# New order of the jobs between the second MLP and the last attention, and the low parts of q and k on GpSimd

## The chip, the cores and the metric

One NeuronCore of a Trainium2 chip runs the whole program. The time is the device time of one execution in microseconds (us); of several executions the median counts. TensorE (PE), VectorE (DVE), ScalarE (ACT), GpSimd (POOL) and SyncE (SP) each work through their own instruction list in order and wait for one another by semaphores. SP only issues DMAs here, and POOL issues some as well.

## The reference, cut to what matters

Four conditional layers on x of 2 batches x 1024 tokens x 256 features, float32. The change lies between the MLP of the second layer and the attention of the fourth:

```python
# end of layer 1: MLP
h = gelu(h @ mlp_w1 + mlp_b1) @ mlp_w2 + mlp_b2 ; x = x_in + h
# layer 2: adapters of rank 8 (a1, bb1, a2, bb2 from the condition)
y = einsum('btd,bdr->btr', x, a1); y = einsum('btr,bdr->btd', y, bb1)
y = gelu(y)
y = einsum('btd,bdr->btr', y, a2); y = einsum('btr,bdr->btd', y, bb2)
x = y + x
# layer 3: norm, 16 heads of 16 features
h = gamma * layernorm(x) + beta
q, k, v = h @ Wqkv.T + bqkv
att = softmax(q @ k.T) / 16 ; out = (att @ v) @ Wp.T + bp ; ...
```

## The kernel before

The order of all work is one list, `SCHED` (lines 86 to 161), of pairs (stage, number). Every engine has a function for the stages in which it takes part, and `run` calls them in the order of the list, so an engine's instruction list is the list of stages cut to its own part. The order on each engine is thus fixed, and a wait holds up all that stands behind it on that engine.

The stages around the change, all of them once for batch 0 and once for batch 1:

- `u1`, `d1`: up and down matmuls of the MLP (L1352, L1374). Batch 1's `d1` parts 24 to 31 are the last. `d1` on POOL adds a bias to X (L800), on DVE adds the result (L2012).
- `x2`: X turned by 16 transposes (L1293), copied by ACT (L1083). `a1`, `g`, `a2`, `f2`: the adapter chain (L1486, L1504, L1486, L1515). ACT copies `a1` and `a2` (L1128) and takes the gelu of `g` (L1133). For `f2` DVE adds four banks to X (L2113) and takes statistics (L1774, L1777), POOL makes the reciprocal deviations (L794, L795), and `fn` normalises on DVE (L1785).
- `n3`: XN turned (L1293). ACT writes each of four tiles twice (L1068), once rounded to float32r as the high part and once whole, and DVE subtracts for the low part (L2134).
- `qk3` j: one tile (128 features x 512 tokens) of q or k, six matmuls (L1529) of three products of high and low parts. Eight jobs for batch 0 (0 to 7), eight for batch 1 (8 to 15). ACT writes the high part (L1123), DVE the low part from the same PSUM bank (L2122) into `PARTS`, which holds four jobs, and two DMAs (L579, L580) store 512 and 256 KB in DRAM: from SP for jobs 0 to 7, from POOL for 8 to 15.
- `v3` j: 12 matmuls (L1540), copied by ACT into `VP` (L1076). Four jobs for each batch.
- `mx` n: two matmuls (L1578) of the pass that finds the row maxima of the scores, reduced by one DVE instruction (L2157). The two pairs of banks in PD alternate, so `mx` n waits until n-2 is reduced. The first 26 (`LEAD`) are done before the first `step`, the other 230 in the steps. `tm` turns a unit's maxima, and SP spreads them (L731).
- `bt`, `bm`: a bias row through the projection. POOL pads `VP` with memsets (L885, L888) in `x2` of batch 1.
- `step` n, 128 of them: energies (L1607), exponentials on ACT (L1154), the sum with the values (L1618), and two `mx`.

Jobs that go through the four banks of PA, all but `mx`, `tm` and the down matmuls, take them in turn: each waits until the job four before it in the list has been evacuated. `g` and `f2` ask for all their four banks before their first matmul.

SP's list has its own order: store jobs 0 to 3; stack 0 (`stack(1)`, four DMAs from DRAM into `STKR`, L700, which wait until jobs 0 to 3 are stored); rows of ones (L708); wait for the MLP's end; stack 1; store jobs 4 to 7; ones; stack 2 (waits until jobs 4 to 7 are stored); ones; then the maxima for the steps. `mx` 0 waits for stack 0. ACT waits before `qk3` j (j of 4 and more) until job j-4 is stored.

## Time and profile before

| what | value |
| --- | --- |
| median of 3 runs | 880.11 us (878.17 to 881.54) |
| the profiled execution | 879.38 us, span 877.5 us |
| mean granted clock of TensorE | 0.977 |
| PE busy | 828.5 us, 94% of the span |
| DVE busy | 682.6 us, 78% |
| ACT busy | 471.6 us, 54% |
| POOL busy | 227.9 us, 26% |
| last down matmul of the second MLP to first energy of the steps | 439.8 to 506.1 us |

How to read it: busy time is summed over an engine's instructions. PE's matmuls are pipelined, so that a record is longer than the distance to the next one. The distance between starts is what a matmul costs. The granted clock is a share of full speed (2.4 GHz at 1.0, 1.2 GHz at 0.5). All positions in time are us from the start of the span.

### The profile page before, as it was taken

The numbers are of one execution on the slowest core, as the hardware profiler recorded it, in microseconds if no ns is written. First come the engines' busy times: TensorE is split into PE (matmuls) and PEld (weight loads), VectorE is DVE, ScalarE is ACT, GpSimd is POOL, SyncE is SP. The second block draws the span as 40 slices with busy tenths as digits, with TensorE's granted clock in tenths as the row PEclk, the third lists the DMA queues.
The fourth block names the chain that finished last, engine by engine and source line by source line (L and its number), as shares of the span: only waits on it lengthen the run. The fifth ranks groups of instructions, "written<-read, shape, count | busy, mean of one in ns | idle before, by whom it ended". The sixth has DMA issues, their size and how long they took to land.

```text
span 877.5 us, 13593 instructions
## 1 busy us (share of the span) xinstructions
PE 828.5 (94%) x5112; PEld 537.5 (61%) x5112; DVE 682.6 (78%) x1155; ACT 471.6 (54%) x857; POOL 227.9 (26%) x377
## 2 busy tenths in 40 slices
PE   5999999999999999997988989999999999999994
PEld 3668888988987998886856633333333433333342
DVE  7998657779558568648358869999999999999377
ACT  4746232243342452343234257888888788888760
POOL 4443412203003003112012620333333333333411
PEclk9999999999999999999989969999999999999996
DMA  8613122110000000000596700505050405010002
GB/s 314 252 49 97 51 96 99 49 53 1 1 1 1 1 1 1 1 1 1 174 201 158 264 1 3 92 21 92 21 93 21 92 21 98 23 25 21 27 25 73
DMA packets 29381, 57.42 MB, mean 65 GB/s; under 512 B 7228, under 2 KB 15152, under 8 KB 29314
## 3 DMA queue, kind: packets, MB, share of 16 engines
q1 hardware_dynamic: 22596, 44.40, 19.4%
q0 software_dynamic: 6720, 12.15, 4.7%
q8 instruction: 41, 0.67, 0.3%
q14 instruction: 24, 0.20, 0.1%
HBM read 39.26 MB, written 14.91 MB: 62 GB/s over the span
## 4 chain that ended last, share of the span: by engine, by line
PE 80%; DVE 11%; ACT 5%; issue 2%; DMA 1%; POOL 1%; SPq 0%; DVEq 0%; ACTq 0%
PE PA L1607 15%; PE PA L1618 15%; PE PD L1374 10%; PE PA L1352 8%; PE PD L1578 7%; PE PA L1463 5%; PE PD L1432 4%; PE PA L1419 3%; PE PA L1529 2%; PE PD L1676 2%; PE PA L1540 2%; PE PA L1293 1%; DVE NMX L2157 1%; PE PA L1453 1%; DVE ST L1774 1%
## 5 line engine op out<-in xcount | busy, mean ns | idle before, releaser
L2157 DVE TENSOR_REDUCE NMX<-PD 128x2 f32<-128x1024 f32 x256 | 302.1, 1222 | 29.2 <-PE PD L1578 24.7
L1154 ACT ACTIVATE R<-PA 128x512 f32<-128x512 f32 x512 | 267.4, 604 | 72.8 <-PE PA L1607 71.2
L1607 PE MATMUL PA<-STKR 50*128 50x512 f32 x512 | 186.1, 455 | 3.8 <-ACT R L1154 2.7
L1607 PEld LDWEIGHTS PA<-STKR 50*128 50x128 f32 x512 | 83.1, 188 | 153.1 <-ACT R L1154 138.8
L1578 PE MATMUL PD<-STKR 48*128 48x512 f32 x512 | 150.2, 456 | 3.3 <-DVE NMX L2157 3.3
L1090 ACT ACTIVATE R<-PA,VEC 128x512 f32<-128x512 f32 x64 | 43.9, 689 | 102.9 <-PE PA L1352 90.4
L1374 PE MATMUL PD<-WHR,HSR 128*128 128x256 f32 x512 | 95.0, 285 | 0.5 <-DVE HSR L1994 0.5
L1374 PEld LDWEIGHTS PD<-WHR,HSR 128*128 128x128 f32 x512 | 82.1, 191 | 5.8 <-issue 1.6
L1352 PE MATMUL PA<-XSR,WHR 128*128 128x512 f32 x256 | 81.1, 398 | 3.9 <-issue 2.0
L1578 PEld LDWEIGHTS PD<-STKR 48*128 48x128 f32 x512 | 62.4, 188 | 21.9 <-DVE NMX L2157 10.9
L1374 PE MATMUL PD<-WLR,HSR 128*128 128x256 f32 x256 | 72.4, 283 | 0.0
L1993 DVE CAST HSR<-R 128x512 fp32r<-128x512 f32 x64 | 28.4, 444 | 56.2 <-ACT R L1090 56.2
L1618 PE MATMUL PA<-R 128*32 128x512 f32 x512 | 70.8, 626 | 0.0
L1618 PE MATMUL PA<-R,W 128*32 128x512 f32 x512 | 68.2, 605 | 0.0
L1352 PEld LDWEIGHTS PA<-XSR,WHR 128*128 128x128 f32 x256 | 45.5, 190 | 14.4 <-issue 7.0
L1994 DVE TENSOR_TENSOR HSR<-R,HSR 128x512 fp32r<-128x512 f32 x64 | 51.8, 810 | 2.2
L800 POOL TENSOR_TENSOR X<-X,BC 128x256 f32<-128x256 f32 x48 | 35.3, 756 | 65.0 <-DVE HSR L1994 53.3
L1352 PE MATMUL PA<-XSR,WLR 128*128 128x512 f32 x128 | 49.9, 390 | 0.0
L1374 PEld LDWEIGHTS PD<-WLR,HSR 128*128 128x128 f32 x256 | 48.9, 191 | 0.0
L1463 PE MATMUL PA<-VR,PTR 128*128 128x256 f32 x384 | 48.3, 284 | 0.0
L1463 PEld LDWEIGHTS PA<-VR,PTR 128*128 128x128 f32 x384 | 47.3, 191 | 0.6
L1102 ACT ACTIVATE R<-PD,NMS 128x1024 f32<-128x1024 f32 x16 | 17.9, 1117 | 54.2 <-DVE NMS L2066 54.1
(326 smaller groups left out, 1268.3 us busy)
## 6 DMA issues: line engine op xcount, KB each, us to landing
STKR<-qk_terms SPq DMA_DIRECT2D x32, 384.0 KB, 8.7
R<-in_l_w SPq DMA_DIRECT2D x8, 1024.0 KB, 5.1
W<-in_w SPq DMA_DIRECT2D x4, 1024.0 KB, 10.2
qk_terms<-PARTS SPq DMA_DIRECT2D x8, 512.0 KB, 3.4
qk_terms<-PARTS POOLq DMA_DIRECT2D x8, 512.0 KB, 3.4
S<-row_reciprocals POOLq DMA_DIRECT2D x56, 64.0 KB, 2.1
X<-in_x SPq DMA_DIRECT2D x4, 512.0 KB, 8.9
qk_terms<-PARTS SPq DMA_DIRECT2D x8, 256.0 KB, 4.5
```

What stands on the lines that cost most here:

```text
L800: i = po.tensor_tensor(x, x, row, ALU.add)
L1090: act.activation(dst, bank(b, tag, c, f_), func, bias=vec(bias, f_)).then_inc(s_aev, 1)
L1154: act.activation(PB[:, n % 2, j, :], PA[:, e % NEB, :], ACT.Exp).then_inc(s_exp3, 1)
L1352: m = pe.matmul(o, parts[w][:, k, f_ * P:(f_ + 1) * P], XS[:, c, x, k, :], start=(n == 0), stop=(n == len(terms) - 1))
L1374: m = pe.matmul(PD[:, (n + t) % 4, 0:D], HS[:, x, f_, t * P:(t + 1) * P], parts[w][:, f_, :], start=(f_ == 0 and (w, x) == TERMS[0]), stop ...
L1432: m = pe.matmul(PDF[:, t % 2, c * HALF:(c + 1) * HALF], QT[q][:, k, t * P:(t + 1) * P], KT[x][:, k, c * HALF:(c + 1) * HALF], start=(n == ...
L1463: m = pe.matmul(o[:, 0:D], PTR[:, x, t % NTURN, kt * P:(kt + 1) * P], V[v][:, kt, :], start=(n == 0), stop=(n == len(terms) - 1))
L1578: i = pe.matmul(PD[:, o + h, :], QS[rows, slot(gg), jj, q0:q0 + P], KS[rows, slot(gg), jj, kc * HALF:(kc + 1) * HALF], start=True, stop=True)
L1607: pe.matmul(PA[:, e % NEB, :], KS[rows, slot(gg), jj, kt * P:(kt + 1) * P], QS[rows, slot(gg), jj, c * HALF:(c + 1) * HALF], start=True, s ...
L1618: i = pe.matmul(PA[32 * j:32 * j + 32, 3, :], VP[b][:, kt, g_ * GH + j, :], PB[:, step % 2, j, :], start=(kt == 0), stop=(kt == NT - 1))
L1994: ve.tensor_tensor(lo, src, hi, ALU.subtract).then_inc(s_split, 1)
L2157: ve.tensor_reduce(out, PD[:, o:o + NROW, :], axis=AX_X, op=ALU.max, negate=True).then_inc(s_mred, 1)
```

## The change

Six edits:

1. Batch 0's `qk3` 0 and 1 come after `d1` 25 and `qk3` 2 and 3 after `d1` 26; before they came after `d1` 23 and 24. `n3` of batch 0 stays behind `d1` 23.
2. Between the MLP and batch 1's `n3` the list has a new order. `v3` 0 stands ahead of `g`, `v3` 1 and 2 ahead of `n3`, `v3` 3 after it; 5 `mx` instead of 9 stand ahead of `n3`.
3. Among `qk3` 8 to 15 there are two `mx` behind each job (before, one or two), and no `mx` is left behind the last `v3` pair.
4. ACT writes each job's q or k twice, the high part and the whole value; POOL subtracts the high part from the whole one in place. DVE has no part in `qk3`.
5. SP stores all 16 jobs. Jobs 8 to 13 stand behind stack 2 and its ones, jobs 14 and 15 behind the first spread of the maxima.
6. The high part of batch 1's `n3` has a buffer of its own (`XH1`); the padding of `VP` is a stage of its own (`vp`) behind `qk3` 7.

```diff
-               NTILE + 5: [("fn", 0)], NTILE + 7: [("n3", 0), ("qk3", 0), ("qk3", 1)],
-               NTILE + 8: [("qk3", 2), ("qk3", 3)]})
+               NTILE + 5: [("fn", 0)], NTILE + 7: [("n3", 0)], NTILE + 9: [("qk3", 0), ("qk3", 1)],
+               NTILE + 10: [("qk3", 2), ("qk3", 3)]})
...
-SCHED += [("x2", 1), ("qk3", 4), ("a1", 1), ("bt", 0), ("g", 1), ("qk3", 5), ("mx", 0), ("bm", 0), ("qk3", 6), ("mx", 1), ("a2", 1), ("mx", 2), ("mx", 3),
-          ("f2", 1), ("qk3", 7), ("mx", 4), ("v3", 0), ("mx", 5), ("v3", 1), ("fn", 1), ("mx", 6), ("v3", 2), ("mx", 7), ("v3", 3),
-          ("mx", 8), ("n3", 1)]
-EARLY = 9
+SCHED += [("x2", 1), ("qk3", 4), ("a1", 1), ("bt", 0), ("v3", 0), ("g", 1), ("mx", 0), ("mx", 1), ("qk3", 5), ("bm", 0), ("a2", 1),
+          ("qk3", 6), ("f2", 1), ("mx", 2), ("fn", 1), ("mx", 3), ("qk3", 7), ("vp", 0), ("v3", 1), ("v3", 2), ("mx", 4), ("n3", 1),
+          ("v3", 3), ("mx", 5)]
+EARLY = 6
...
-    SCHED += [("qk3", QJOBS + j), ("mx", EARLY)]
-    EARLY += 1
-    if EARLY >= UNIT + 2 and ("tm", 0) not in SCHED:
-        SCHED.append(("tm", 0))
-    elif j % 2 and j < QJOBS - 1:
+    SCHED.append(("qk3", QJOBS + j))
+    for i in range(2):
+        if EARLY >= UNIT + 2 and ("tm", 0) not in SCHED:
+            SCHED.append(("tm", 0))
         SCHED.append(("mx", EARLY))
         EARLY += 1
...
+            XH1 = at("XH1", R0 + 12288, [P, KB, T])
...
-        X3 = [[XH0[:, :, :], XTR[:, 0]], [XTR[:, 0], XTR[:, 1]]]
+        X3 = [[XH0[:, :, :], XTR[:, 0]], [XH1[:, :, :], XTR[:, 1]]]
...
                 for j in jobs:
-                    evacuated(sp, *qk3_job(j))
+                    sp.wait_ge(s_low3, j + 1)
                     store_parts(sp, j)
...
             ones_rows(2)
+            store(range(QJOBS, 2 * QJOBS - 2))
             for m in range(NUNIT):
...
+                if m == 0:
+                    store(range(2 * QJOBS - 2, 2 * QJOBS))
...
             def qk3(j):
-                if j >= QJOBS:
-                    evacuated(po, *qk3_job(j))
-                    store_parts(po, j)
+                high, low = parts(j)[:, 0], parts(j)[:, 1]
+                evacuated(po, *qk3_job(j))
+                po.tensor_tensor(low, low.bitcast(F32), high.bitcast(F32), ALU.subtract).then_inc(s_low3, 1)
...
-                act.activation(parts(j)[:, 0], full_bank(b, tag, side, c, k), ACT.Identity,
-                               bias=vec(("q3_b", "k3_b")[side], k)).then_inc(s_hi, 1)
+                o = bank(b, tag, side, c, k)
+                for dst in (parts(j)[:, 0], parts(j)[:, 1].bitcast(F32)):
+                    i = act.activation(dst, o, ACT.Identity, bias=vec(("q3_b", "k3_b")[side], k))
+                i.then_inc(s_aev, 1)
```

## Rows read from the trace of the kernel before

**Rows 1.** Stretches of 4 us: busy per engine, granted clock, DMA share, GB/s

```profile
416.00:420.00 4.00, 4.00 (x13) 3.14 (x12) 1.36 (x3) 0.69 (x2) 0.00 (x0) 0.63 0.06 17
...
440.00:444.00 4.00, 4.00 (x39) 2.87 (x36) 0.57 (x3) 2.76 (x5) 3.85 (x3) 1.00 1.04 160
...
456.00:460.00 4.00, 2.62 (x21) 1.80 (x22) 4.00 (x6) 0.00 (x0) 0.00 (x0) 0.75 1.04 386
...
512.00:516.00 4.00, 4.00 (x20) 1.64 (x16) 2.15 (x3) 2.10 (x4) 0.00 (x0) 0.50 0.02 6
...
528.00:532.00 4.00, 4.00 (x27) 1.33 (x27) 3.75 (x4) 3.41 (x7) 0.00 (x0) 1.00 0.00 0
```

**Rows 2.** PE in order of time, MLP's end: start, length, line, [idle before, releaser]

```profile
415.66 0.47 PE L1529 MATMUL PA<-XH,WQH 128*128 128x512 f32 x1 [4.03 <-DVE XSR L2134]
...
439.84 1.91 PE L1293 MATMUL PA<-ident,X 128*128 128x128 f32 x16
```

**Rows 3.** The chain that ended last, `qk3` 0 to 3: start, us, what

```profile
415.66 4.29 PE PA L1529 x12
...
425.80 2.75 PE PA L1529 x12
```

**Rows 4.** ACT in order of time: last evacuation of batch 0's `n3`

```profile
415.02 0.81 ACT L1068 ACTIVATE XT<-PA,PAR 128x512 f32<-128x512 f32 x1
```

**Rows 5.** PE in order of time, 445 to 506 us

```profile
445.19 1.15 PE L1504 MATMUL PA<-R,LB 8*128 8x256 f32 x16 [0.70 <-DVE DG L2137]
...
456.26 1.15 PE L1515 MATMUL PA<-LB,R 8*128 8x256 f32 x16
...
475.89 0.74 PE L1529 MATMUL PA<-XSR,WQH 128*128 128x512 f32 x2 [2.29 <-DVE XSR L2134]
...
487.94 0.50 PE L1578 MATMUL PD<-STKR 48*128 48x512 f32 x2
488.37 0.72 PE L1529 MATMUL PA<-XSR,WQH 128*128 128x512 f32 x2
...
489.92 0.50 PE L1578 MATMUL PD<-STKR 48*128 48x512 f32 x2
...
501.87 0.49 PE L1578 MATMUL PD<-STKR 48*128 48x512 f32 x2
...
503.92 0.73 PE L1578 MATMUL PD<-STKR 48*128 48x512 f32 x4
...
506.07 0.69 PE L1607 MATMUL PA<-STKR 50*128 50x512 f32 x3
```

**Rows 6.** DVE in order of time: adds of `f2`, and `fn`

```profile
457.96 2.48 DVE L2113 TENSOR_TENSOR X<-PA,X 128x512 f32<-128x512 f32 x4
...
466.73 2.67 DVE L1785 TENSOR_SCALAR XN<-X,MV,RST 128x256 f32<-128x256 f32 x8
```

**Rows 7.** The reductions of all `mx`, from the page: busy, mean ns

```profile
L2157 DVE TENSOR_REDUCE NMX<-PD 128x2 f32<-128x1024 f32 x256 | 302.1, 1222 | 29.2 <-PE PD L1578 24.7
```

**Rows 8.** POOL by line and shape: its two operations on 128 x 512

```profile
L911 POOL TENSOR_TENSOR S<-UO,S 128x512 f32<-128x512 f32 x7 | 8.9, 1276 | 12.5 <-DMA S<-row_reciprocals 12.5
...
L876 POOL TENSOR_TENSOR R<-R,S 128x512 f32<-128x512 f32 x4 | 7.1, 1776 | 12.8 <-DVE R L1956 12.8
```

**Rows 9.** DVE's subtraction L1994 in 404 to 430 us: ns min/median/max

```profile
L1994 DVE TENSOR_TENSOR HSR<-R,HSR x6: 693/693/1107, 406.6 to 425.8; 128x512 fp32r<-128x512 f32 x6
```

**Rows 10.** POOL beside the longest of these, in order of time

```profile
425.50 0.85 POOL L800 TENSOR_TENSOR X<-X,BC 128x256 f32<-128x256 f32 x1 [1.09 <-DVE HSR L1994]
```

**Rows 11.** SP's DMA issues of stacks 0 and 1, in order of time

```profile
434.29 1.76 SPq L700 DMA_DIRECT2D STKR<-qk_terms  x4
...
440.03 6.81 SPq L700 DMA_DIRECT2D STKR<-qk_terms  x4
```

**Rows 12.** DMA issues from the page (KB each, us to landing)

```profile
STKR<-qk_terms SPq DMA_DIRECT2D x32, 384.0 KB, 8.7
```

**Rows 13.** Landing times of all stores of L579

```profile
DMA to landing us min/median/max: 2.8/3.4/11.2
```

More of the change, by code:

```diff
@@ L265, in evacuations @@
     for _, tag, *_ in jobs:
-        by_dve = int(tag in ("ad", "gc", "wt", "wv", "q", "k", "v1", "p", "o", "qk3", "f2", "bt", "bm"))
+        by_dve = int(tag in ("ad", "gc", "wt", "wv", "q", "k", "v1", "p", "o", "f2", "bt", "bm"))
         seen[by_dve] += 1
@@ L528, in build @@
         s_exp1 = sem("probs1_ready")
-        s_hi = sem("qk_high_ready")
+        s_low3 = sem("qk_low_ready")
         s_w3high = sem("last_attention_weights_high_ready")
@@ L881, in x2, with v_padding @@
                     po.memset(ONES[:, :].bitcast(F32), 1.0).then_inc(s_ones, 1)
-                    return
+            def v_padding(_):
                 po.wait_ge(s_dfull, DJ[(1, "w21", NT - 1)] + 1)
@@ L930, in _ @@
                  "d0": prebias_in_mlp(0, lambda b: BG[:, b, :]), "h0": normed("h0", 1e-6, rms=True), "att": att,
-                 "pr": normed("pr", 1e-6, rms=True), "d1": prebias_in_mlp(1, lambda b: BC[:, MB2, :]), "x2": x2,
+                 "pr": normed("pr", 1e-6, rms=True), "d1": prebias_in_mlp(1, lambda b: BC[:, MB2, :]), "x2": x2, "vp": v_padding,
                  "f2": normed("f2", 1e-5), "qk3": qk3, "step": step, "end": normed("end", 1e-5)})
@@ L2114, in f2 @@
                 stats(b, lambda h: evacuated(ve, b, "f2", 2 * h + 1))
-            def qk3(j):
-                b, tag, side, c, k = qk3_job(j)
-                n = AJ[(b, tag, side, c, k)]
-                high, low = parts(j)[:, 0], parts(j)[:, 1]
-                bias = VC[("q3_b", "k3_b")[side]] + k
-                ve.wait_ge(s_hi, j + 1)
-                ve.scalar_tensor_tensor(low, PA[:, n % 4, :], VEC[:, bias:bias + 1], high.bitcast(F32), ALU.add,
-                                        ALU.subtract).then_inc(s_aevd, 1)
             def last_weights(_):
@@ L2236, in _ @@
                  "ao": att("ao"), "pr": pr, "d1": d1,
-                 "f2": f2, "fn": lambda b: normalise("f2", b, True), "qk3": qk3, "n3": last_halves, "w3": last_weights, "bt": bias_turned, "bm": bias_projected, "mx": reduce_max,
+                 "f2": f2, "fn": lambda b: normalise("f2", b, True), "n3": last_halves, "w3": last_weights, "bt": bias_turned, "bm": bias_projected, "mx": reduce_max,
                  "tm": turned_max, "step": step, "hd": heads_turned, "hx": heads_back, "p3": p3, "st": last_stats, "ea": end_scaled, "eb": end_sum})
```

## The prediction

> **What bounds the kernel now.** I read the stretches of 4 us first. TensorE is busy nearly everywhere except in one transition, from the end of the second MLP to the first energy, and in one hole ahead of it. From 416 to 420 it works at a mean clock of 0.63, and a later stretch holds only 2.62 us of work in 4 [rows 1]; there are several such. Next, PE in order of time: batch 0's n3 has ended at 411.6, and the next matmul starts at 415.66, after 4.03 us of idle, because qk3 0 needs the halves that ACT and DVE make from n3. The MLP ends and x2 starts at 439.84; the first energy is at 506.07 [rows 2, 5]. So the transition takes 66.2 us. From 506 on, the program is a fixed chain of 128 steps that the change leaves alone, so an earlier first energy is worth its full amount at the end, unless the clock there differs.
>
> **Term A: qk3 0 to 3 behind d25 and d26.** Three up jobs and two down parts now follow n3. The two spots of qk3 show the price of the clock: 12 matmuls took 4.29 us after the hole and 2.75 us without one [rows 3], so the hole costs 4.03 + 1.5 us. The cover is not perfect: u28 needs the bank of n3's first tile. ACT's n3 work of eight passes ends at 415.83 at 0.66 us a pass [rows 4], so the first two passes are done at 411.8, when PE has left the transposes; some 0.3 us stay. The up jobs of 1.38 us (six matmuls at 0.229) then just meet the other banks. Gain about 5.4 (4.5 to 5.8): x2 at 434.4.
>
> **Term B: x2 to f2.** Before, f2 started 16.4 us after x2 (439.84 to 456.26) [rows 2, 5]. Now x2 (1.66), qk3 4 (1.37), a1 (1.0), bt and v3 0 follow until 440.6. g asks for four banks and the last is v3 0's, so it starts when ACT has copied v3 0, 441.5, 0.9 idle, where before it started 5.35 after x2 [rows 5], which would be 439.8 now. Then mx 0 needs stack 0. Stores 2 and 3 follow ACT's two passes and POOL's subtraction and are ready at 427.5 and 428.9; with 768 KB each at 386 GB/s, 2.0 us [rows 1], stack 0 is issued near 433.0, against 434.29 [rows 11]. A stack is 4 x 384 KB [rows 12], at 160 GB/s [rows 1] 9.8 us, and it lands near 444.5. PE reaches mx 0 at 442.6: 1.9 idle, a wait that did not exist, and all of PE's list is behind it. Then mx 0, mx 1, qk3 5, bm, a2, qk3 6, some of it at half clock after these gaps: a2 near 450, qk3 6 ends at 451.6. f2's last bank is qk3 6's, which ACT frees after two passes (0.7 + 0.66), so f2 starts at 453.4 (452.6 to 455). That is 19 us after x2: this part loses 2.6. The gain so far is 2.9.
>
> **Term C: f2 to fn's end.** Before: 456.26 to 469.40, 13.1 us [rows 5, 6]. Adds and statistics take 7.0 us after f2's start (DVE then turned to the low part of qk3 7 at 463.8, which was 7.5 after f2; without a pause between add and add 7.0); then stood that low part (0.7) and two reductions, now one. With one reduction of 1.2 [rows 7] and fn's 2.7 [rows 6] the new time is 10.9. POOL has room: its rstd works sit ahead of qk3 7's low part. Gain 2.2; fn ends at 464.3.
>
> **Term D: fn's end to qk3 8.** Before 6.5 us (to 475.89, of them 2.29 idle) [rows 5, 6], while ACT and DVE turned n3 into halves. Now v3 3 and mx 5 stand in that wait. PE: last half of n3 0.8, v3 3 1.6, mx 5 0.4, and up to 1.5 for half clock (the hole of 4.03 cost that much [rows 3]; PE is idle near 460 to 461 and 462 to 464 waiting for mx 2's reduction and fn). The halves needed by qk3 8 are ready at 467.8. So qk3 8 starts at 468.6, 4.3 after fn: gain 2.2 (1.5 to 3).
>
> **Term E: qk3 8 to the first energy.** Before 30.2 us (475.89 to 506.07). A job takes 1.55 on PE and an mx 0.43 (487.94, 488.37, 489.92 [rows 5]). Two reductions on DVE take 2.44 at 1.222 each, a little less back to back [rows 7]. PE needs 1.55 + 0.43 + 0.43 = 2.41, with the second mx waiting until the reduction of the pair before has ended. The two chains are about equal, and I take 2.43 us a job. 8 x 2.43 = 19.4, tm 0.3, then four v3 and mx at 2.05 (501.87 to 503.92 [rows 5]) 8.2, and 0.3 for the last evacuation: 28.2. The mx pairs that stood behind v3 7, from 503.92 to the first energy at 506.07, are gone; but three mx and one v3 more follow n3 than before. Gain 2.0 (0 to 3).
>
> Sum: 5.4 - 2.6 + 2.2 + 2.2 + 2.0 = 9.2, so the first energy at 496.8. In the profiled execution 879.38 - 9.2 = 870.2; the median stood 0.73 above the profiled one, so 870.9.
>
> **What is costed at nothing.** *POOL's low part.* No row shows this operation on 128 x 512. The nearest, a product on 128 x 512, takes 1.28 us beside DVE's reductions and 1.78 in another place [rows 8]. Against a period of 2.43 both fit. I take 1.35; a faster one gains nothing, for nobody on PE waits for it. It would have to exceed 2.4 to set the pace. *ACT's second pass* (0.66) has room in 2.43, and its cost at f2 is in term B. *DVE* loses 16 low parts of 0.75, which is what makes room for two reductions. *SP.* Store 7 is ready at 463, lands at 466, stack 2 is issued then and lands at 477; stores 8 to 11 follow in the same queue at 2.0 each (479.5, 481.6, 483.6, 485.7). ACT wants job 8 stored at 479.7 for qk3 12, and job 11 at 487 for qk3 15, so waits are 0.6 at most and PE has four banks of room. The spread of the maxima lands near 490, needed at 496.8. *vp* (4.4 us on POOL at 463 to 467) is ahead of low part 8, needed at 471.5.
>
> GpSimd beside DVE: DVE's subtraction of 0.693 took 1.107 beside an add on POOL at its longest [rows 9, 10]. The Trainium skill, "GPSIMD Engine Reference", section 8 "Key points", says that the two share SBUF interfaces and collide for DVE instructions in a two-port mode or with two SBUF inputs. By that rule fn's and n3's operations beside low 7 and vp would be stretched by up to 0.4 each for the overlapped two or three, the trace agrees, and the sum would be 0.5 to 1 smaller: 871.6. The reductions read PSUM and keep 1.22, so I leave it in the range.
>
> **Rivals.**
>
> *Clock at the steps.* In the first steps, as at 512 to 516, PE works at clock 0.50 though it is busy throughout: 20 matmuls in 4 us, where 528 to 532 has 27 [rows 1]. That lasts to about 522, some 12 us that give a quarter less, and PE's waits for the first exponentials stand ahead of it. Estimate from these counts: 3 to 4.5 us lost. The new end of the transition has less idle; if the clock stays, 866.4. Against: the waits for the first exponentials stay. Chance 0.15.
>
> *A smaller gain: the queue.* Stores 4 to 7 are behind stack 1, 8 to 13 behind stack 2, all in SP's queue. A stack issue was held 6.81 us [rows 11], and stores behind one landed after 11.2 instead of 3.4 [rows 13]. If store 7 is late by 4 us (chain or POOL's list), stack 2 lands at 481, job 11 at 490, qk3 15 is evacuated at 491.5 and the end moves by 3 to 4 us: 874.5. The same size comes from a clock at half through most of 445 to 470. Chance 0.23. The Trainium skill, "DMA: Bandwidth & Descriptors", section "Issuing engines are not separate DMA queues", says that DMAs of all issuers run on the same 16 engines and interleave, so that a second issuer saves only issue time. By it moving the stores costs nothing but POOL's 1.3 us; in the trace a store behind a stack in one queue waits it out, and no row shows one from POOL beside a stack.
>
> *No change.* Only the MLP hole is won and the waits at mx 0, g, f2 and fn eat it: 876 to 884. Chance 0.08.
>
> *Slower.* More and longer gaps (1.9 at mx 0, 1.5 at f2, 1.6 and 1 at mx 4 and n3) leave the clock at half when the dense part starts, and it stays there as in 510 to 522. PE's 2.41 a job nearly doubles, 4.2 (1.8 more), and v3 with its mx goes from 2.05 to 3.4 (1.4 more). Over the whole stage 14.4 + 5.6 = 20, so 890.9. It decides from seven to eight jobs on: 9.2 + 4.4 = 13.6, over 1.8. Against: the fall behind the hole of 4.03 was over by 420, for the 12 matmuls at 425.80 ran at full price [rows 3]. Chance 0.05.
>
> **How the numbers follow.** The forecast holds 0.49, 868 to 873.5 around 870.9. A measurement can tell 0.5% here (4.4 us), so faster is below 875.7. With the clock case 0.15 and most of the queue case, faster 0.83; same 0.11; slower 0.06. The range leaves out the last two cases: 865.5 to 876.
>
> **What would show it.** No idle over 1 us on PE behind n3 of batch 0 and x2 at 434 to 435 (A). PE idle ahead of mx 0 with a DMA as releaser, and f2 at 452.6 to 455 (B). fn's end 11 us after f2 (C). Less than 0.5 idle ahead of qk3 8 (D). Jobs 8 to 15 at 2.4 us, POOL's L-line at 1.3 to 1.8 us (E). First energy at 495 to 499. The prediction falls if PE waits inside jobs 8 to 15 for ACT or a store, if POOL's subtraction takes over 2.4 us, or if the steps are slower than 2.5 us after the start.

## The result and the profile after

The changed kernel takes 873.53 us (median of 20 runs, 872.63 to 877.29), the kernel before 877.90 us in the 20 runs beside it (874.47 to 881.54). The ratio is 0.9957, 95% interval 0.9942 to 0.9971: faster by 0.43%, less than half of the 1.0% that was forecast (870.9), inside the range, and by its ratio just on the "no change" side of the 0.5% bound, which had a chance of 0.11. In two of the kernels below, e7 and e10, one disturbed run is in the count and the median, and not in the ratio. The profiled execution has a span of 871.3 us at a mean clock of 0.984, where the one of before had 877.5 at 0.977.

The page of the changed kernel, with its busy times:

```profile
span 871.3 us, 13609 instructions
PE 824.4 (95%) x5112; PEld 536.8 (62%) x5112; DVE 675.7 (78%) x1139; ACT 479.6 (55%) x873; POOL 237.9 (27%) x377
```

DVE has lost 7 us, ACT and POOL have gained 8 and 10, as the change says. PE has lost 4, though it does the same matmuls; the mean clock is higher (0.984 against 0.977). Now the transition, PE in order of time, the rows that answer to [rows 2, 5] (start, length, [idle before it, releaser]):

```profile
411.81 0.70 PE L1358 MATMUL PA<-XSR,WHR 128*128 128x512 f32 x2 [0.32 <-ACT XT L1072]
...
434.37 1.91 PE L1299 MATMUL PA<-ident,X 128*128 128x128 f32 x16
441.29 1.15 PE L1510 MATMUL PA<-R,LB 8*128 8x256 f32 x16 [0.84 <-ACT R L1080]
444.98 1.22 PE L1584 MATMUL PD<-STKR 48*128 48x512 f32 x4 [2.54 <-DMA STKR<-qk_terms]
454.98 1.15 PE L1521 MATMUL PA<-LB,R 8*128 8x256 f32 x16 [1.51 <-ACT PARTS L1129]
...
469.14 3.67 PE L1299 MATMUL PA<-ident,XN 128*128 128x128 f32 x16 [5.45 <-DVE XN L1791]
...
475.60 0.50 PE L1535 MATMUL PA<-XH,WQH 128*128 128x512 f32 x1
...
504.71 0.70 PE L1613 MATMUL PA<-STKR 50*128 50x512 f32 x3 [0.46 <-ACT W L1080]
```

Read against the forecast's five terms (L1584 is `mx`, L1521 `f2`, L1299 `x2` and `n3`, L1535 `qk3`, L1613 the energy):

| stretch | before | forecast | after | gain forecast | gain measured |
| --- | --- | --- | --- | --- | --- |
| A: start to `x2` | 439.84 | 434.4 | 434.37 | 5.4 | 5.5 |
| B: `x2` to `f2` | 16.4 | 19.0 | 20.6 | -2.6 | -4.2 |
| C: `f2` to the end of `fn` | 13.1 | 10.9 | 15.4 | 2.2 | -2.3 |
| D: end of `fn` to `qk3` 8 | 6.5 | 4.3 | 5.2 | 2.2 | 1.3 |
| E: `qk3` 8 to the first energy | 30.2 | 28.2 | 29.1 | 2.0 | 1.1 |
| first energy at | 506.07 | 496.8 | 504.71 | 9.2 | 1.4 |

The transition gave 1.4 us instead of 9.2; the span is shorter by 6.2. The other 4.8 lie behind the first energy, in steps that the change leaves alone. So there are two questions: where the transition's 7.8 us went, and where the steps' 4.8 came from.

DVE at `fn` in the changed kernel, the rows that answer to [rows 6], and POOL beside it:

```profile
461.95 1.19 DVE L2154 TENSOR_REDUCE NMX<-PD 128x2 f32<-128x1024 f32 x1
463.06 7.32 DVE L1791 TENSOR_SCALAR XN<-X,MV,RST 128x256 f32<-128x256 f32 x8
470.30 2.35 DVE L2154 TENSOR_REDUCE NMX<-PD 128x2 f32<-128x1024 f32 x2
```

```profile
463.44 1.25 POOL L897 TENSOR_TENSOR PARTS<-PARTS 128x512 fp32r<-128x512 f32 x1
464.64 1.79 POOL L889 MEMSET R<- 128x2048 f32 x1
466.49 0.34 POOL L892 MEMSET R<- 128x128 f32 x1
466.69 1.85 POOL L889 MEMSET W<- 128x2048 f32 x1
468.60 0.34 POOL L892 MEMSET W<- 128x128 f32 x1
```

The eight instructions of `fn` took 2.67 us before [rows 6] and take 7.32 now. They have the same operands, and DVE waits for nobody: its records are long. The times of a single one, of the changed kernel by line in 455 to 475 us (ns min/median/max):

```profile
L1791 DVE TENSOR_SCALAR XN<-X,MV,RST x8: 395/402/3205, 463.1 to 470.0; 128x256 f32<-128x256 f32 x8
```

and the two long ones, in order of time:

```profile
463.38 3.21 DVE L1791 TENSOR_SCALAR XN<-X,MV,RST 128x256 f32<-128x256 f32 x1
466.51 2.18 DVE L1791 TENSOR_SCALAR XN<-X,MV,RST 128x256 f32<-128x256 f32 x1
```

Five take 0.4 us, one 0.48, one 2.18 and one 3.21. The long ones end at 466.59 and 468.69, each 0.15 us after the end of a large memset (466.44 and 468.54), and the one of 0.48 ends 0.15 after the last small memset. From 463.44 to 468.94 POOL works almost without a break, 5.5 us, and `fn` grew by 4.65. PE stands for 5.45 us ahead of `n3`, and then works at half clock. The stretches of the changed kernel, columns as in [rows 1]:

```profile
444.00:448.00 4.00, 3.02 (x9) 2.02 (x9) 2.19 (x2) 0.48 (x1) 0.00 (x0) 0.53 0.88 151
448.00:452.00 4.00, 4.00 (x24) 2.18 (x23) 0.59 (x2) 1.31 (x3) 1.27 (x1) 0.62 1.05 167
...
464.00:468.00 4.00, 0.00 (x0) 0.00 (x0) 4.00 (x2) 0.00 (x0) 3.94 (x4) 1.00 0.53 197
468.00:472.00 4.00, 2.85 (x14) 2.86 (x15) 4.00 (x8) 1.70 (x3) 0.88 (x2) 0.51 0.78 138
472.00:476.00 4.00, 4.00 (x20) 3.57 (x19) 2.74 (x5) 4.00 (x7) 0.00 (x0) 0.63 1.01 154
...
508.00:512.00 4.00, 4.00 (x19) 1.52 (x19) 2.33 (x2) 2.29 (x6) 0.91 (x2) 0.63 0.00 0
512.00:516.00 4.00, 4.00 (x30) 1.67 (x26) 3.72 (x4) 3.49 (x8) 0.00 (x0) 0.94 0.01 4
```

From 464 to 468 DVE is busy for 4.00 us with two instructions. Twice a wait of PE is followed by 1.2 GHz (0.53 and 0.51). The last two lines are the steps: PE is close to full clock from 512 on (0.94), where before showed 0.50 at 512 [rows 1] and still

```profile
516.00:520.00 4.00, 4.00 (x20) 1.64 (x16) 2.29 (x3) 2.10 (x4) 0.00 (x0) 0.50 0.00 0
520.00:524.00 4.00, 4.00 (x21) 1.68 (x17) 2.47 (x4) 2.10 (x4) 0.00 (x0) 0.64 0.00 0
```

(the kernel before, same columns). In 4 us PE started 20 matmuls there, and 30 in the changed kernel.

### The profile page after: what moved, and what is told of

Its sections match the earlier page's. It is cut to its first block, busy times and chain, and to the rows that moved or that the text cites. A ratio compares the mean times of both kernels' runs of the same rounds, so it can differ in the third digit from the quotient of the medians.

```text
span 871.3 us, 13609 instructions
## 1 busy us (share of the span) xinstructions
PE 824.4 (95%) x5112; PEld 536.8 (62%) x5112; DVE 675.7 (78%) x1139; ACT 479.6 (55%) x873; POOL 237.9 (27%) x377
## 4 chain that ended last, share of the span: by engine, by line
PE 79%; DVE 10%; ACT 4%; DMA 2%; issue 2%; POOL 1%; SPq 1%; DVEq 0%; ACTq 0%
PE PA L1613 15%; PE PA L1624 15%; PE PD L1380 9%; PE PA L1358 8%; PE PD L1584 7%; PE PA L1469 5%; PE PD L1438 4%; PE PA L1425 3%; PE PA L1535 2%; PE PA L1299 2%; PE PD L1682 1%; PE PA L1459 1%; DVE ST L1780 1%; DMA STKR<-qk_terms 1%; PE PA L1546 1%
## 5 line engine op out<-in xcount | busy, mean ns | idle before, releaser
L1613 PE MATMUL PA<-STKR 50*128 50x512 f32 x512 | 183.8, 449 | 4.2 <-ACT R L1160 2.7
L1613 PEld LDWEIGHTS PA<-STKR 50*128 50x128 f32 x512 | 81.9, 185 | 151.3 <-ACT R L1160 141.8
L1584 PE MATMUL PD<-STKR 48*128 48x512 f32 x512 | 148.1, 452 | 3.0 <-DMA STKR<-qk_terms 2.5
L1584 PEld LDWEIGHTS PD<-STKR 48*128 48x128 f32 x512 | 60.7, 186 | 22.2 <-DVE NMX L2154 9.0
```

What stands on the lines that cost most here:

```text
L1584: i = pe.matmul(PD[:, o + h, :], QS[rows, slot(gg), jj, q0:q0 + P], KS[rows, slot(gg), jj, kc * HALF:(kc + 1) * HALF], start=True, stop=True)
L1613: pe.matmul(PA[:, e % NEB, :], KS[rows, slot(gg), jj, kt * P:(kt + 1) * P], QS[rows, slot(gg), jj, c * HALF:(c + 1) * HALF], start=True, s ...
```

## The experiments

Theory 1: what is missing from the transition is DVE's `fn` beside GpSimd's work (C), and `mx` 0, which waits for its stack (B). Theory 2: the order is at its limit, and something else becomes late where one of these is mended. For the steps: their length follows the clock in their first 24 us, which only e7's edit aims at.

| kernel | median (runs) | ratio to before, 95% | first energy | span behind it | clock, first 12 us and next 12 |
| --- | --- | --- | --- | --- | --- |
| before | 877.90 (20) | | 506.07 | 371.4 | 0.63, 0.80 |
| after | 873.53 (20) | 0.9957 (0.9942 to 0.9971) | 504.71 | 366.6 | 0.86, 1.00 |
| e1 | 870.27 (7) | 0.9928 (0.9901 to 0.9954) | 499.90 | 368.6 | 0.72, 1.00 |
| e2 | 872.99 (8) | 0.9942 (0.9920 to 0.9963) | 499.67 | 371.4 | 0.62, 0.81 |
| e3 | 878.17 (12) | 1.0007 (0.9987 to 1.0028) | 508.68 | 367.3 | 0.72, 1.00 |
| e4 | 871.52 (11) | 0.9942 (0.9918 to 0.9966) | 500.47 | 367.0 | 0.86, 1.00 |
| e5 | 867.29 (6) | 0.9893 (0.9862 to 0.9924) | 496.75 | 370.1 | 0.72, 1.00 |
| e6 | 876.68 (12) | 0.9991 (0.9968 to 1.0015) | 504.98 | 369.4 | 0.67, 0.90 |
| e7 | 877.38 (12) | 1.0004 (0.9973 to 1.0035) | 507.32 | 365.7 | 1.00, 1.00 |
| e8 | 876.83 (12) | 0.9990 (0.9973 to 1.0007) | 507.90 | 369.8 | 0.67, 0.91 |
| e10 | 866.28 (6) | 0.9880 (0.9848 to 0.9913) | 497.00 | 368.5 | 0.58, 0.99 |
| e11 | 862.88 (5) | 0.9838 (0.9813 to 0.9863) | 493.80 | 367.2 | 0.86, 1.00 |
| e12 | 874.81 (12) | 0.9967 (0.9947 to 0.9987) | 504.93 | 366.9 | 0.86, 1.00 |

The last three columns are of the one profiled execution; "first energy" is the start of the first matmul of the steps, the clock that of two stretches of 12 us from there. The intervals of neighbouring kernels often overlap (after, e1, e2, e4 and e12 do), so what one edit is worth is read from the first energy, and the total only supports it. The first energy has its own scatter: in the six kernels whose lists are alike up to `x2` (after, e1, e4, e5, e10, e11) it starts between 433.74 and 434.89, so a difference below about 1 us says nothing.

**e1, the changed kernel with the padding written early**, while DVE and GpSimd are both free:

```diff
-SCHED += [("x2", 1), ("qk3", 4), ("a1", 1), ...
-          ("qk3", 6), ("f2", 1), ("mx", 2), ("fn", 1), ("mx", 3), ("qk3", 7), ("vp", 0), ("v3", 1), ...
+SCHED += [("x2", 1), ("vp", 0), ("qk3", 4), ("a1", 1), ...
+          ("qk3", 6), ("f2", 1), ("mx", 2), ("fn", 1), ("mx", 3), ("qk3", 7), ("v3", 1), ...
```

> The changed kernel with one move: the padding of VP (four memsets on GpSimd, 4.3 us) goes back to its old place behind x2 of batch 1, where VectorE has nothing to do. Main theory (GpSimd's work beside fn stretched fn from 2.67 to 7.32 us): fn takes 3 to 4 us (the low part of qk3 7, 1.25 us, still lies beside it), fn ends near 467 instead of 470.4, TensorE's idle of 5.45 us ahead of n3 falls below 2.5, and the first energy comes at 500 to 502 instead of 504.7; the median is 3 to 5 us below the changed kernel's 873.5. Rival (fn was late for another reason, the late f2 or a late reciprocal deviation, and GpSimd only happened to be busy): fn stays above 6 us and the time at 873. Second rival (the wait for stack 0 ahead of mx 0 is what costs): nothing changes before f2, and the gain is below 1 us.

DVE in order of time, and then POOL beside it, of e1:

```profile
462.27 3.73 DVE L1791 TENSOR_SCALAR XN<-X,MV,RST 128x256 f32<-128x256 f32 x8
```

```profile
462.66 1.25 POOL L897 TENSOR_TENSOR PARTS<-PARTS 128x512 fp32r<-128x512 f32 x1
```

With the memsets gone, 1.25 us of GpSimd's work remain beside `fn`, and `fn` takes 3.73: 1.06 over its 2.67. The first energy comes 4.8 us earlier than in the changed kernel, more than the 3.6 by which `fn` shrank, since `f2` was also 0.8 earlier in this execution. The median falls by 3.3. Four memsets of 4.3 us, moved and not removed, cost this kernel more than the whole transition had gained.

**e3, the converse: the kernel before with its memsets moved to that place**, behind the rstd of `f2`, and nothing else changed:

```diff
-          ("f2", 1), ("qk3", 7), ("mx", 4), ...
+          ("f2", 1), ("vp", 0), ("qk3", 7), ("mx", 4), ...
```

> The kernel before with one move: the padding of VP (four memsets on GpSimd, 4.3 us) stands behind the reciprocal deviations of f2, so that it lies beside fn on VectorE. Everything else is as before. Main theory (the memsets hold up VectorE's fn): fn takes 5.5 to 7.5 us instead of 2.67, the first energy is 3 to 5 us later, the median 3 to 5 us above the kernel before. Rival (GpSimd and VectorE do not collide at such sizes, or by some tenths only, as the prediction had it with 0.4 for two or three operations): fn stays below 4 us and the time within 1.5 us.

`fn` by line, of e3 (ns min/median/max), and POOL in order of time:

```profile
L1786 DVE TENSOR_SCALAR XN<-X,MV,RST x8: 396/404/2202, 467.1 to 471.4; 128x256 f32<-128x256 f32 x8
```

```profile
465.68 1.80 POOL L886 MEMSET R<- 128x2048 f32 x1
467.54 0.36 POOL L889 MEMSET R<- 128x128 f32 x1
467.74 1.86 POOL L886 MEMSET W<- 128x2048 f32 x1
469.66 0.36 POOL L889 MEMSET W<- 128x128 f32 x1
```

`fn` starts at 467.11, so 2.9 us of memsets lie beside it, and it takes 4.66 us instead of 2.67. One instruction of 0.4 us took 2.20, about what one large memset and one small one take. The first energy came 2.6 us later (508.68; 0.4 of it was there at `x2`, and `fn` is 2.0), while this execution's steps were 4.1 us shorter. The ratio is 1.0007, and its interval holds no change, where I had expected 3 to 5 us. So the stretch of `fn` is shown in the trace of a kernel that has nothing else of the change; in the total it is not. In the profiled execution the steps ran at a better clock (0.72, 1.00), which hides it; whether that holds for the median is not shown.

**e4 and e5: `mx` 0 and 1 behind `a2`**, in the changed kernel (e4) and with e1's edit as well (e5):

```diff
-          ("v3", 0), ("g", 1), ("mx", 0), ("mx", 1), ("qk3", 5), ("bm", 0), ("a2", 1),
+          ("v3", 0), ("g", 1), ("qk3", 5), ("bm", 0), ("a2", 1), ("mx", 0), ("mx", 1),
```

> The changed kernel with mx 0 and mx 1 behind a2 instead of behind g, so that TensorE meets the wait for stack 0 some 3 us later, when it has landed. Theory of the stack's wait: the idle of 2.54 us ahead of mx 0 goes, half clock near 445 to 451 shrinks, f2 starts at 449.5 to 452 instead of 454.98, and the first energy comes 3 to 5 us sooner than 504.7. fn stays at about 7 us, since the padding still lies beside it. The median is 3 to 5 us below 873.5. Rival (that wait is cover for nothing else and the chain through gelu and the banks sets f2): f2 moves by less than 1.5 us and the time stays at 872.5 to 873.5.

> The changed kernel with both moves at once: the padding of VP back behind x2 of batch 1, and mx 0 and mx 1 behind a2. Theory: the two losses lie one behind the other on the same chain (x2 to f2, then f2 to fn's end), so they add: f2 at 451 to 452, fn 3.7 us long, fn's end near 463.5 instead of 470.4, first energy at 496.5 to 498 instead of 504.7, median 866 to 868. Rival (beyond 4 to 5 us something else is late next, above all stack 2 and the stores behind it in SP's queue, or the halves of n3): first energy no sooner than 499, median 869 to 870, with TensorE idle inside qk3 8 to 15.

PE in order of time, 438 to 452 us, of e4:

```profile
440.81 1.15 PE L1510 MATMUL PA<-R,LB 8*128 8x256 f32 x16 [0.84 <-ACT R L1080]
442.69 0.47 PE L1535 MATMUL PA<-XH,WQH 128*128 128x512 f32 x1 [0.73 <-ACT R L1139]
447.70 0.73 PE L1584 MATMUL PD<-STKR 48*128 48x512 f32 x4
451.54 1.15 PE L1521 MATMUL PA<-LB,R 8*128 8x256 f32 x16 [1.51 <-ACT PARTS L1129]
```

The wait for the stack is gone, and `f2` starts at 451.54, 3.4 us earlier: 0.5 because `x2` is earlier in this execution, 1.8 because one wait of 0.73 for the gelu stands where 2.54 for the stack stood, and the rest from a shorter stretch at half clock. The first energy comes 4.2 earlier, though `fn` is nearly as slow as in the changed kernel (7.04). The median falls by 2.0 only, where I had expected 3 to 5. With both moves, e5's first energy is at 496.75, 7.96 us ahead of the changed kernel's; e1 and e4 alone gave 4.81 and 4.24. Counted from `x2`, which differs by up to 1 us between these executions, it is 8.48 together and 4.56 and 3.77 alone. So the costs of the two faults add (8.33), and the forecast's 496.8 is reached in the profile, though not by its terms: `x2` to `f2` takes less than forecast, since the wait that was part of it is gone, and the three stretches behind it take more (11.7, 4.5 and 29.7 us). The median is 867.29.

**e2 and e6: the MLP's part alone, and all but that part.** e2 is the kernel before with the first edit of the change, e6 the changed kernel with that edit undone:

```diff
-               NTILE + 5: [("fn", 0)], NTILE + 7: [("n3", 0), ("qk3", 0), ("qk3", 1)],
-               NTILE + 8: [("qk3", 2), ("qk3", 3)]})
+               NTILE + 5: [("fn", 0)], NTILE + 7: [("n3", 0)], NTILE + 9: [("qk3", 0), ("qk3", 1)],
+               NTILE + 10: [("qk3", 2), ("qk3", 3)]})
```

> The kernel before with edit 1 alone: qk3 0 and 1 behind d1 25, qk3 2 and 3 behind d1 26. Main theory (term A is worth its 5.4 us also at the end, and the rest of the change gave it back): x2 at 434.4, first energy 4 to 5.5 us ahead of 506.07, median 4 to 5.5 us below the kernel before, so as fast as or faster than the whole change. A smaller gain is possible only where store 3 comes later than before and stack 0 is not there for mx 0; stores here leave VectorE at 425 to 427, so stack 0 should land by 443, ahead of mx 0 at 444. Rival (the transition is bound by the stacks' DMAs, which start no sooner): the first energy moves by less than 2 us and the time stays within 2 us of the kernel before.

> The changed kernel with edit 1 undone: qk3 0 to 3 back behind d1 23 and 24, the rest of the change in. Theory (part of the 5.4 us won in the MLP was spent on the new wait for stack 0): x2 comes at 439.8 again, stack 0 lands near 445, so the wait ahead of mx 0 is gone or below 0.5 us, f2 is only 2.5 to 3.5 us later than in the changed kernel, and with the long fn the first energy comes at 507 to 508.5: the rest of the change alone is 1 to 2.5 us slower than the kernel before, 878 to 880. Rival (the gain of edit 1 carries through in full in the changed kernel): first energy at 510, median 879 and more. Second rival (the rest of the change is worth its own 3 to 4 us, as forecast): 873 to 875.

e2 moves the first energy by 6.4 us and gives 872.99: the first edit alone is worth as much as all six. e6 has its first energy at 504.98, within 0.3 us of the changed kernel's, where I had expected 507 to 508.5, and its ratio to the kernel before is 0.9991 (0.9968 to 1.0015): in the total the rest of the change alone shows no gain. So in the changed kernel nothing of term A's 5.4 us arrives. The reason is in the same place of both traces. SP of e6, and PE:

```profile
435.63 1.76 SPq L700 DMA_DIRECT2D STKR<-qk_terms  x4
```

```profile
446.57 1.15 PE L1510 MATMUL PA<-R,LB 8*128 8x256 f32 x16 [0.84 <-ACT R L1080]
447.96 0.73 PE L1584 MATMUL PD<-STKR 48*128 48x512 f32 x4 [0.24 <-DMA STKR<-qk_terms]
...
455.21 1.15 PE L1521 MATMUL PA<-LB,R 8*128 8x256 f32 x16 [1.51 <-ACT PARTS L1129]
```

PE comes to `mx` 0 when its stack lands anyway (0.24 of wait). In the changed kernel PE is 5.3 us earlier (`g` at 441.29), but stack 0 is issued only 2.2 us earlier (433.46), PE waits 2.54 us, works at 0.53 and 0.62 for 8 us, and reaches `f2` at 454.98, which is 0.23 before e6: 2.3 us of the 5.3 went into the wait and 2.75 into the slower way from `mx` 0 to `f2` (10.0 us against 7.25). In e2 PE does `qk3` 5 ahead of `mx` 0 and waits 0.40. The medians of the changed kernel and e6 are still 3.1 us apart, which their first energies do not tell; the steps' clock differs between the two profiled executions (0.86, 1.00 against 0.67, 0.90).

**e8 and e12: the low parts of q and k back on DVE, on top of e5.** e8 undoes the fourth edit (with it, ACT's second pass, and SP waits for DVE). e12 is e8 with one wait more:

```diff
             def qk3(j):
-                evacuated(po, *qk3_job(j))
-                po.tensor_tensor(low, low.bitcast(F32), high.bitcast(F32), ALU.subtract).then_inc(s_low3, 1)
+                pass
...
             def step(n):
...
                     po.wait_ge(s_bp3, 1)
+                    po.wait_ge(s_low3, 16)
```

> The kernel e5 (both moves on top of the change) with the last part of the change undone: VectorE makes the low parts of q and k again, ScalarE's projections go back to their old form, and GpSimd makes none. Theory (VectorE's 3.1 us against 2.5 us set the eight jobs 8 to 15, as the rows of before and after show): the jobs take 3.1 us each instead of 2.49, fn returns to 2.7 us since nothing of GpSimd lies beside it, f2 comes some 0.6 us earlier, and the first energy lies at 500 to 501 instead of e5's 496.75; median 870 to 872 beside e5's 867.3. Rival (the low parts on GpSimd bring nothing, since they cost VectorE what they spare it): first energy within 1 us of 496.75, median within 1 us of e5's.

> The kernel e8 with one wait added on GpSimd: its sixteen additions of the last projection's bias (11 us, due only at the end) stay behind the sixteenth low part, where they lie in before and in after. In e8 nothing held them there once GpSimd had no low parts, and they ran from 460.98 to 473.6 beside fn, the halves and the first low parts. Theory (fn's 5.63 us in e8 came from these additions, and a job of 8 to 15 costs VectorE 3.0 us instead of 2.49): fn takes 2.7 us again, ends at 463.2, qk3 8 lies at 468 to 470, the jobs take 3.0 us each, the first energy comes at 500.5 to 503, median 870 to 873. Rival (the additions were harmless and e8's 5 us came from the order of the low parts alone): fn stays above 5 us or the first energy within 1.5 us of e8's 507.90, median 875 to 877.

(The last line of the diff is e12's alone.) DVE's `fn` in 450 to 472 us, ns min/median/max, in e8 and then in e12:

```profile
L1788 DVE TENSOR_SCALAR XN<-X,MV,RST x8: 403/808/923, 460.6 to 465.4; 128x256 f32<-128x256 f32 x8
```

```profile
L1789 DVE TENSOR_SCALAR XN<-X,MV,RST x8: 403/404/406, 460.6 to 462.8; 128x256 f32<-128x256 f32 x8
```

and what GpSimd did in e8 at that time:

```profile
460.98 12.67 POOL L803 TENSOR_TENSOR X<-X,BC 128x256 f32<-128x256 f32 x16
```

I had overlooked these. The sixteen additions of the last bias stood behind GpSimd's stores in the kernel before, and stand behind its low parts in the changed one; they need only `fn`. Take the queue in front of them away and they run beside `fn` and the halves. One wait removes them (e12), and nothing else differs: `fn` falls from 5.63 to 2.66 us and the first energy from 507.90 to 504.93. From `fn`'s end to there both take 41.7 us, so the whole 2.97 us is `fn`'s. The median goes from 876.83 to 874.81; the two ratios overlap (0.9973 to 1.0007, 0.9947 to 0.9987). That is the cleanest pair on the contention: the same instruction, the same start to 0.01 us, with and without GpSimd beside it. DVE's further rows of e8 show who suffers and who does not:

```profile
467.94 1.21 DVE L2160 TENSOR_REDUCE NMX<-PD 128x2 f32<-128x1024 f32 x1
469.07 1.01 DVE L2137 TENSOR_TENSOR XSR<-XT,XH 128x512 fp32r<-128x512 f32 x1
470.71 2.34 DVE L2137 TENSOR_TENSOR XSR<-XT,XH 128x512 fp32r<-128x512 f32 x2 [0.63 <-ACT XT L1071]
```

A reduction out of PSUM keeps its 1.21 us. A subtraction of two SBUF tensors, 0.69 us in e12, takes 1.01, 1.20 and 1.00 beside GpSimd's additions (the last row merges two of them).

For the fourth edit itself e12 against e5 counts: 874.81 against 867.29, and 504.93 against 496.75. The theory had 500.5 to 503 and 870 to 873, so the low parts on GpSimd are worth more than I gave them. Jobs 8 to 15 take 3.04 us each in e12 (DVE's low part at 475.40, 478.44, 481.37, 484.41, 487.55) and 2.49 in e5: 4.4 us over eight. `f2` is 1.6 later, and the part from `fn`'s end to `qk3` 8 takes 6.7 us instead of 4.5: there DVE has a low part to make ahead of `n3`'s halves, and PE is at 0.62. `fn` itself is 0.95 shorter than in e5. The rest is a stretch at half clock at 492 to 496. So GpSimd's low part earns 8.2 us in this stretch, the one us or so that it costs `fn` already taken off.

**e7, work in the hole ahead of the first exponentials.** The kernel before, with eight matmuls that compute nothing of the result, so that PE does not stand idle there:

```diff
                 energy(n, 2)
+                if n == 0:
+                    for _ in range(8):
+                        pe.matmul(PA[:, 3, :], KS[0:KFULL, slot(0), 0, 0:P], QS[0:KFULL, slot(0), 0, 0:HALF],
+                                  start=True, stop=True)
```

> The kernel before with eight extra matmuls of 50 rows x 512 columns into the bank that the first sum with the values clears anyway, placed where TensorE waits for the first exponential (1.79 us idle). Nothing else is changed. Theory (the slow first steps, some 12 us at clock 0.50, come from the idle ahead of them, and their length is what makes runs of one kernel differ by some us): the hole is below 0.5 us, the clock falls for a shorter time or not at all, the steps take 367 us instead of 371.4, the median is 1 to 3.5 us below the kernel before and the runs lie closer together. Rival (the fall is not set off by that hole, for instance by the work of few rows itself): the clock at 512 to 520 is 0.50 as before and the time within 0.5 us, or longer by up to 1 us where the eight matmuls hold up the next energy.

Stretches of e7:

```profile
508.00:512.00 4.00, 4.00 (x21) 2.25 (x23) 2.63 (x4) 3.99 (x7) 3.27 (x5) 1.00 0.00 0
512.00:516.00 4.00, 4.00 (x30) 1.63 (x23) 3.28 (x3) 2.92 (x7) 0.00 (x0) 1.00 0.02 6
516.00:520.00 4.00, 4.00 (x30) 1.43 (x27) 3.85 (x5) 3.45 (x8) 0.00 (x0) 1.00 0.00 0
```

In the profiled execution the clock stays at 2.4 GHz and the steps take 365.7 us, the shortest of all. But the eleven runs behind the ratio fall into two groups, six from 871.7 to 875.5 us at mean clocks of 0.983 and more, and five from 879.3 to 883.8 at 0.979 and less, and the ratio is 1.0004. It shows what a full clock is worth at this place, and not a way to get it: inconclusive.

**e10 and e11, a version that goes further.** Both are the changed kernel with `vp` early and the adapter chain ahead of the max jobs (`r2` is the rstd of `f2` as a stage of GpSimd's own; the max jobs left over stand between the last `v3`):

```diff
+SCHED += [("x2", 1), ("vp", 0), ("qk3", 4), ("a1", 1), ("bt", 0), ("g", 1), ("qk3", 5), ("a2", 1), ("f2", 1),
+          ("qk3", 6), ("qk3", 7), ("r2", 1), ("fn", 1), ("v3", 0), ("v3", 1), ("mx", 0), ("v3", 2), ("mx", 1), ("n3", 1),
+          ("v3", 3), ("mx", 2), ("bm", 0), ("mx", 3)]
```

and e11 against e10 (stack 2 now behind the first spread of the maxima):

```diff
+SCHED += [("x2", 1), ("vp", 0), ("qk3", 4), ("a1", 1), ("bt", 0), ("g", 1), ("qk3", 5), ("a2", 1), ("mx", 0), ("f2", 1),
+          ("r2", 1), ("qk3", 6), ("mx", 1), ("qk3", 7), ("fn", 1), ("v3", 0), ("mx", 2), ("v3", 1), ("mx", 3), ("n3", 1),
+          ("v3", 2), ("mx", 4), ("v3", 3), ("mx", 5), ("bm", 0)]
...
-            stack(NSLOT)
-            ones_rows(2)
             store(range(QJOBS, 2 * QJOBS - 2))
...
                     store(range(2 * QJOBS - 2, 2 * QJOBS))
+                    stack(NSLOT)
+                    ones_rows(2)
```

> The changed kernel with a new list between x2 and the jobs of batch 1: the padding behind x2, v3 0 behind the chain, and a1, g, a2, f2 with only qk3 4 and 5 between them; qk3 6 and 7, v3 0 to 2 and mx 0 and 1 fill TensorE while VectorE does f2's adds, statistics and fn; GpSimd's low parts of 6 and 7 stand ahead of the reciprocal deviations of f2; the last 26 mx are spread so that none is alone at the end. Theory (the chain from x2 to fn's end is what sets the transition, and it can be cleared of the waits for stack 0, for the banks and for GpSimd): f2 at 445 to 446.5, fn 2.7 us long and ended at 455 to 457, qk3 8 near 460, first energy at 489 to 492, median 858 to 862. Rival (SP's queue: stack 2 lands near 474 and ACT waits for the stores of jobs 8 to 11): TensorE stalls inside the jobs or v3 4 to 7, first energy at 493 to 497, median 863 to 866.

> The kernel e10 (chain ahead of the max jobs, padding written early) with three orders changed: fn's rstd goes ahead of the low parts 6 and 7 on GpSimd, the max jobs 0 to 3 are spread over four gaps of the chain, and on SyncE stack 2 and the rows of ones are issued behind the first stores of jobs 8 to 15, which in e10 waited 8.2 us behind stack 2. Theory (e10 lost at rstd, 3.6 us, and at the queue): fn ends at 456.5 to 457.5, qk3 8 at 462, the jobs keep 2.5 us each, first energy 489 to 493, median 859 to 863, and ScalarE's waits for stores are gone. Rival (VectorE has no time left to give in this stretch, or the half clock costs TensorE what the order spares): first energy 495 to 497, median 865 to 867.

e10's first energy at 497.00 and its median are at the upper edge of the rival. What it lost, DVE and then SP in order of time:

```profile
456.29 2.84 DVE L1795 TENSOR_SCALAR XN<-X,MV,RST 128x256 f32<-128x256 f32 x8 [3.61 <-POOL RST L802]
```

```profile
464.87 1.75 SPq L704 DMA_DIRECT2D STKR<-qk_terms  x4
466.66 1.09 SPq L712 DMA_DIRECT2D STKR<-ONES  x2
467.93 8.20 SPq L583 DMA_DIRECT2D qk_terms<-PARTS  x1
```

GpSimd's low parts 6 and 7, which wait for PE, stood in front of the rstd that `fn` wants (3.61 us). And the first store behind stack 2 was held in SP for 8.20 us, after which ACT waited up to 2.23 us for stores. In e11 the issue of store 8 takes 0.36 us and ACT waits for no store. Its `fn` takes 4.61 us, for two low parts (2.8 us) lie beside it. It starts at 453.86, where that of before started at 466.73 [rows 6]. The first energy is at 493.80, just past the 489 to 493 that I gave, and the median is 862.88 us, ratio 0.9838 (0.9813 to 0.9863), inside the 859 to 863: the fastest kernel here, 1.6% under the one before and 1.2% under the changed one.

## Why the prediction was right, and where it was wrong

**The time.** 873.53 lies 2.6 us above the forecast of 870.9, inside 865.5 to 876. But that it came so close is luck, for the agreement hides errors of opposite sign: the transition gained 1.4 us instead of 9.2, and the profiled steps gained 4.8 instead of nothing. A third one lies in the start: I took the gain off 880.11, the median of three runs, where twenty runs of the same kernel have 877.90. Against that the gain of the medians is 4.4 us, 4.8 short of the forecast. By its mechanism the outcome is that of the third rival, "only the MLP hole is won and the waits at `mx` 0, `g`, `f2` and `fn` eat it", which had 0.08, with part of the first, the clock at the steps, on top. My most likely case did not happen.

**A held**, to 0.1 us, with the idle of 0.32 ahead of u28 that I had from ACT's passes.

**B: the mechanism was right, the size short by 1.6.** Stack 0 was issued at 433.46 (forecast 433.0) and PE was released at 444.98 (444.5), idle 2.54 (1.9). From there to `f2` I had 8.9 us; it took 10.0, at 0.53 and 0.62, where I had written "some of it at half clock" and priced too little. (The forecast of 444.5 does not follow from its two written terms, 433.0 and 9.8; it comes out with the 1.76 us of issuing [rows 11], which I left unsaid.) I should have drawn the other conclusion as well: a wait on a DMA that does not move with PE takes back what is won in front of it. e6 shows that, and e4 that the order alone avoids it.

**C was the step that failed.** I had 10.9 us for `f2` to the end of `fn`; it took 15.4. Up to `fn`'s start the working holds: 463.06 is 8.1 after `f2`, 8.2 by my sum. What was mis-sized is the contention: "stretched by up to 0.4 each for the overlapped two or three", from [rows 9, 10], where a subtraction of 0.693 took 1.107 beside one addition of 0.85. What the runs showed in its place: `fn` grows by 0.7 to 0.85 of the time that GpSimd works beside it on memsets and low parts, not by a fixed sum per instruction.

| kernel | GpSimd's work beside `fn` | `fn` | over 2.67 |
| --- | --- | --- | --- |
| before, e2, e12 | none | 2.67, 2.67, 2.66 | 0 |
| e1 | 1.25 (a low part) | 3.73 | 1.06 |
| e3 | 2.9 (memsets) | 4.66 | 1.99 |
| after | 5.5 (a low part, memsets) | 7.32 | 4.65 |
| e8 | all of it (additions) | 5.63 | 2.96 |

The single instructions say how. In the traces of after, e1, e3, e4, e5, e6, e8 and e11, 24 instructions of this `fn` are longer than 0.45 us, and every one of them ends 0.14 to 0.16 us after the end of an instruction of GpSimd. An instruction of `fn` was held until GpSimd's ended, and sometimes over two of them, as the one of 3.21 us was. So the length of GpSimd's instructions sets the price here. It also explains e8: there one instruction of `fn` comes through with each addition, every 0.73 us instead of every 0.32, and seven times 0.41 is 2.9 us. Small work on GpSimd held nobody: in e10 a GpSimd instruction on 128 x 4 lies beside `fn` for 1.17 us, and each instruction of `fn` takes 0.41.

I read "up to" from a row in which GpSimd's neighbour was itself short, and took the size of that pair for a bound. The trace of the kernel before had a longer pair, with the very instruction of [rows 8] on GpSimd's side:

```profile
63.14 1.50 DVE L1993 CAST XSR<-R 128x512 fp32r<-128x512 f32 x1
```

```profile
62.58 1.78 POOL L876 TENSOR_TENSOR R<-R,S 128x512 f32<-128x512 f32 x1 [5.47 <-DVE R L1956]
```

The same cast takes 0.42 us at the median, so 1.08 us were lost in one instruction. In the change description I also had all that was needed: `vp` behind `qk3` 7 is the one edit that puts 4.4 us of GpSimd beside `fn` (I placed it at 463 to 467, and it came at 464.64 to 468.94). I named it as a neighbour of `fn` and priced it at 0.4 for two or three operations, and otherwise asked only whether low part 8 would be late.

What the Trainium skill says stands beside this. The Trainium skill, "GPSIMD Engine Reference", section "Key points", has the sharing and the two kinds of DVE instruction that it hits. The Trainium skill, "VectorE: DVE Perf Modes", section "The perf-mode tier table", lets an fp32 `tensor_scalar` from SBUF run at twice the rate, which takes both SBUF read ports, and gives PSUM a single port. By that rule `fn` and the halves are hit and the reductions are not, and the traces agree: 0.40 to 3.2 us, 0.69 to 1.20, and 1.19 to 1.22 unchanged. Neither section gives the size.

**D and E: right in kind, 0.9 short each.** D had 1.5 us for the half clock; the sixteen transposes took 3.67 at 0.51, and the wait ahead of them was 5.45, where I had 1 to 1.6. E's job took 2.49 where I had 2.43. GpSimd's subtraction took 1.29 (1.35 taken). From `fn`'s end to the first energy it is 34.3 us in the changed kernel, 33.9 in e1 and 34.2 in e5, and the forecast had 32.5: this part of the error does not depend on the two faults.

**SP's queue was no cause.** ACT and PE wait for no store in jobs 8 to 15 of the changed kernel; store 8 was issued at 480.03 in 0.38 us. The rival was real, but at another place: it struck e10, where the jobs came 12 us earlier behind the same stack. In e1 and e5 ACT also waits for a store, up to 1.62 and 1.78 us, and PE waits for none of it.

**The steps' clock.** In the table of the experiments the span behind the first energy goes from 365.7 to 371.4 us, and goes mostly with the clock of its first 24 us: 371.4 at 0.63 and 0.80 and again at 0.62 and 0.81, 366.6 to 367.2 at 0.86 and 1.00, 365.7 at 1.00. It is not the only thing: e5 has 370.1 and e3 367.3 at the same 0.72 and 1.00. Some of the difference lies at the other end, where from 350 to 360 us behind the first energy the clock is 0.83 in e5, 0.91 in the kernel before and 1.00 in e1. Between the runs of one kernel the time goes with the clock too. Of 82 runs of the kernel before, taken beside the experiments, 31 had a mean clock of 0.977 or less, with a median of 879.60, and 20 had 0.983 or more, with 875.04. Of the changed kernel's 20 runs none was at 0.977 or less, and the 14 at 0.983 or more have 873.28. At a good clock in both, a rough match since the transition is part of the mean, the change is worth 1.8 us, which agrees with the 1.4 of the transition in the profile. The other 2.6 of the 4.4 us between the medians is that runs of the lower clock no longer appear. That the change causes this is not shown. e2, with the MLP's part alone, has 0.62 and 0.81 in its profile, and e4, with all edits, had four of its eleven runs at 0.979 or less. Which wait decides it stays open; e7 was meant to settle it and did not.

## What to carry to other kernels

Before work is moved to GpSimd, or within its list, look at what DVE does in the same microseconds. Where DVE casts or scales an SBUF tensor, or takes two of them, count the whole of GpSimd's busy time on large tensors as lost to DVE; put such work beside DVE's reductions out of PSUM or into its idle time, and hold back what GpSimd would start early for nobody. And before a hole ahead of a DMA wait is credited, ask whether the DMA moves as well: here 5.4 us won in front of a stack were gone at `f2`, 20 us later. Judge a small change in such a kernel by the start of the next long stage, beside the total, since the span behind that start differed by up to 4.8 us between kernels whose steps are the same, while the start itself scatters by about 1 us.
